# Dilated attention in a decoder layer: 32 tile products replaced by 8 full-array products on block-diagonal weights

## The reference

```python
B, N, D = x.shape                                  # 16, 128, 256
w, r, H, hd = (SEG, DILATION, NUM_HEADS, HEAD_DIM) # 64, 2, 16, 16
nseg = Np // w                                     # 2 segments
s = w // r                                         # 32 tokens of a head in a segment
xs = x.reshape(B, nseg, w, H, hd).transpose(0, 1, 3, 2, 4)
offsets = jnp.arange(H) % r                        # even heads see even tokens, odd heads odd ones
idx = offsets[:, None] + jnp.arange(s)[None, :] * r
g = jnp.take_along_axis(xs, idx[None, None, :, :, None], axis=3)
scores = jnp.einsum('bnhqd,bnhkd->bnhqk', g, g) * scale
attn = jax.nn.softmax(scores, axis=-1)
out = jnp.einsum('bnhqk,bnhkd->bnhqd', attn, g)
```

## Time and profile before

| | |
|---|---|
| Median of three executions | 625.38 us |
| Profiled execution: span from its first to its last instruction | 719.4 us |
| Profiled execution: its own time outside that span | not given by the page |
| PE busy in the span | 563.9 us (78%) |
| DVE, ACT, POOL busy | 368.4, 330.1, 390.5 us |
| PE busy from 120 to 180 us (three steps) | 49.2 of 60 us |
| Mean granted clock of TensorE over the span | 0.915 of 2.4 GHz |

### The profile page before, as it was taken

One profiled execution on the slowest core, in us unless ns is written; L12 is line 12 of the kernel. 1 busy time (PEld: TensorE's weight loads), 2 busy tenths in 40 slices (PEclk: granted clock), 3 DMA queues, 4 the chain that ended last, 5 costly groups with the idle time before them and its releaser, 6 DMA issues.

```text
span 719.4 us, 17476 instructions
## 1 busy us (share of the span) xinstructions
PE 563.9 (78%) x5097; PEld 414.4 (58%) x5098; DVE 368.4 (51%) x1527; ACT 330.1 (46%) x1204; POOL 390.5 (54%) x599
## 2 busy tenths in 40 slices
PE   3768787888878888888306889988998888985995
PEld 2445454544555554444105777777777776774884
DVE  1537566666677566666402444444444444443453
ACT  2445555455455455456003555555555554553012
POOL 5443445545544455545551666766666666665432
PEclk9789999999999899999556999999999999998899
DMA  9999996111111111112285554555555454554994
GB/s 206 277 275 365 342 339 231 69 59 73 68 50 64 55 73 73 65 66 74 99 308 182 155 165 150 160 156 167 152 164 159 143 157 142 164 160 148 425 418 145
DMA packets 83069, 121.31 MB, mean 169 GB/s; under 512 B 13779, under 2 KB 72669, under 8 KB 80992
## 3 DMA queue, kind: packets, MB, share of 16 engines
q1 hardware_dynamic: 64128, 78.46, 36.3%
q0 software_dynamic: 14016, 38.44, 14.7%
q10 hardware_dynamic: 4896, 4.03, 1.7%
HBM read 56.07 MB, written 69.01 MB: 174 GB/s over the span
## 4 chain that ended last, share of the span: by engine, by line
PE 54%; issue 12%; ACT 12%; DVE 9%; DMA 6%; ACTq 3%; POOL 2%; SPq 1%; another core or an unknown queue 0%; DVEq 0%; POOLq 0%
PE bank L793 14%; PE bank L809 9%; ACT pr L870 7%; PE bank L611 5%; PE bank L785 5%; PE bank L601 4%; PE bank L803 3%; PE bank L661 3%; DMA out<-fin 3%; PE bank L744 2%; DMA wall<-results 2%; DVE nmax L1024 2%; PE bank L619 2%; ACTq L296 1%; DVE tg L1218 1%
## 5 line engine op out<-in xcount | busy, mean ns | idle before, releaser
L556 POOL DMA_INDIRECT results<-ys,wcol x152 | 150.1, 988 | 25.8 <-POOL pscrap L545 22.0
L530 POOL DMA_INDIRECT queues<-x,xidx x128 | 129.1, 1009 | 36.9 <-issue 36.5
L793 PE MATMUL bank<-wall,xtT 128*128 x616 | 127.1, 330 | 0.7 <-issue 0.7
L870 ACT ACTIVATE pr<-bank,nmax 128x128 f32<-128x128 f32 x256 | 90.9, 370 | 29.1 <-DVE nmax L1024 29.1
L1218 DVE SCALAR_TENSOR_TENSOR tg<-th,bank 128x96 f32<-128x96 f32 x154 | 39.1, 254 | 125.3 <-ACT th L957 96.9
L793 PEld LDWEIGHTS bank<-wall,xtT 128*128 128x128 f32 x616 | 98.4, 194 | 1.4 <-issue 1.3
L963 ACT ACTIVATE ys<-bank,wcol 128x256 f32<-128x256 f32 x152 | 71.9, 473 | 54.6 <-PE bank L809 36.6
L809 PE MATMUL bank<-wall,hT 96*128 x304 | 94.5, 392 | 0.0
L785 PE MATMUL bank<-ident,xt 128*128 128x128 f32 x310 | 63.3, 286 | 35.4 <-DMA xt<-queues 24.1
L785 PEld LDWEIGHTS bank<-ident,xt 128*128 128x128 f32 x310 | 59.0, 197 | 49.9 <-DMA xt<-queues 25.1
L876 ACT COPY prT<-bank 128x512 f32<-128x512 f32 x64 | 38.5, 601 | 88.9 <-PE bank L611 86.2
(11 more groups left out here) (178 smaller groups left out, 947.2 us busy)
## 6 DMA issues: line engine op xcount, KB each, us to landing
xt<-queues SPq DMA_DIRECT2D x162, 160.0 KB
results<-zeros SPq DMA_DIRECT2D x16, 1024.0 KB
wall<-results SPq DMA_DIRECT2D x16, 1024.0 KB, 12.7
queues<-zeros SPq DMA_DIRECT2D x32, 160.0 KB, 4.9
wall<-in_L_ffn_w_gate SPq DMA_DIRECT2D x4, 768.0 KB
wall<-in_L_ffn_w_up SPq DMA_DIRECT2D x4, 768.0 KB
wall<-in_L_ffn_w_down SPq DMA_DIRECT2D x4, 768.0 KB
results<-ys,wcol POOLq DMA_INDIRECT x152
```

The costliest lines, as they stand in the source:

```text
L530: pool.indirect_dma_start(xg, bass.IndirectOffsetOnAxis(ap=xidx[:, par, k:k + 1], axis=0), x2[:, par, :], None, bounds_check=last_row, oob ...
L556: pool.indirect_dma_start(yr, bass.IndirectOffsetOnAxis(ap=wcol[:, u, 1:2], axis=0), ys[:, u, :], None, bounds_check=last_y, oob_is_err=Fa ...
L793: ins = pe.matmul(bank[2 + u % 2][:, 0:2 * INTER].rearrange("p (g i) -> p g i", g=2), xtT[:, u % 2, kk, :], wall[:, bass.ds(e, GU)].rearrange(
L870: ins = act.activation(pr[:, g % 2, q, :], pS[g % 2][:, q * P:(q + 1) * P], ACT.Exp, bias=nmax[:, 4 * g + q:4 * g + q + 1], accum_out=den[ ...
```

## The change

`eAT` becomes 128 partitions x 8 pairs x 128 columns and is set to zero once, on POOL, among the constants (one more constant, so `B_CONST` goes from 27 to 28). DVE transposes with four instructions, one for each partition group, each writing its 32x32 blocks to the columns of its own group, so that `eAT[:, j, :]` is block-diagonal. In step 0 DVE waits for `B_CONST` first. PE then forms the sums of a pair for all four groups with one product over the full array: stationary `eAT[:, j, :]` (128x128), moving the 32 columns of `gm`. The other places of the 128x128 operand are zero. The scores (L640) stay as they are.

```diff
-B_CONST = FIRST_CONST + 23
-N_CONST = 49
+B_CONST = FIRST_CONST + 24
+N_CONST = 50
...
-        eAT = sb("eAT", [P, PAIRS, GR])
+        eAT = sb("eAT", [P, PAIRS, P])
...
+            put(pool.memset, eAT[:, :, :].rearrange("p j k -> p (j k)"), 0.0)
             put(pool.memset, kP[:, :, :, :, :].rearrange("p a m q k -> p (a m q k)"), 0.0)
...
                     for j in range(PAIRS):
-                        for g in range(NG):
-                            ins = pe.matmul(pA[GR * g:GR * (g + 1), j * 32:(j + 1) * 32],
-                                            eAT[GR * g:GR * (g + 1), j, :],
-                                            gm[GR * g:GR * (g + 1), par, j * 32:(j + 1) * 32],
-                                            start=True, stop=True, tile_position=(GR * g, GR * g))
+                        ins = pe.matmul(pA[:, j * 32:(j + 1) * 32], eAT[:, j, :], gm[:, par, j * 32:(j + 1) * 32],
+                                        start=True, stop=True)
                     ins.then_inc(peA.sem, 1)
...
                     dve.reciprocal(rA[:, :], dA[:, :]).then_inc(s, 1)
-                    dve.transpose(flat2(eAT), flat2(eA)).then_inc(s, 1)
+                    if isinstance(a, int) and a == 0:
+                        dve.wait_ge(consts, B_CONST)
+                    for g in range(NG):
+                        rows = slice(GR * g, GR * (g + 1))
+                        ins = dve.transpose(eAT[rows, :, GR * g:GR * (g + 1)], eA[rows, :, :])
+                    ins.then_inc(s, 1)
```

## The result

The kernel with the change takes 661.16 us (median of four executions, 660.92 to 661.41), the kernel before beside it on the same chip 625.78 us (624.9 to 626.59). The ratio is 1.0572, with a 95% interval from 1.0556 to 1.0587: 35.4 us slower. The forecast was 648.5 us, within 630 to 660. The direction is right, the size is not, and 661.16 lies outside the range.

The account below looks back on a forecast made before the run. The chain V0, L661, T1, ACT's copy, exponentials, T2 and next scores was taken to set each step. 15 steps x 1.2 us (1.08 + 0.15, rounded) = 18.0, plus step 0's 5.1: 625.4 + 23.1 = 648.5 us, range 630 to 660.

Parts of the forecast that it names:

- The drip: L661's passes in small bursts with 0.45 us issue gaps, steps 3 to 15; taken as recording's price, absent from timed runs.
- The rival beside which the Trainium skill's: L661's slow bursts are the kernel's own, perhaps instruction fetches, and 96 fewer instructions end them: 600 us, chance 0.14.
- The span of 697 us: Forecast length of the changed kernel's profiled execution, shorter than the 719 us before, though the timed kernel takes longer.
- PE's products: In L661, 16 passes at 0.11 us, 1.76 us, replace 0.68, so T1 comes 1.08 us later each step.
- DVE's transposes: Three more ahead of yB at 0.32 us each: yB 0.96 to 1.31 us later, 0.96 taken; V0 0.15 later.
- the slack of V0: About a microsecond between yB and V0's start, used up by the transposes; V0 then 0 to 0.4 us later.
- The half clock: PE's stretch at clock 0.50 following L661, seen in the first profile; forecast to be gone after the change.
- half clock in all steps: Rival: L661's products run at half clock in every step, 3.55 us, 2.9 later instead of 1.1; 675 us, chance 0.04.
- Step 0: First step: zeroing 0.95 us, transposes 1.35, passes at half clock 2.8 more; sum 5.1 us.
- POOL's path: POOL's root of r and indirect DMAs, moved by the transposes' 0.96; bounds the step's cost from below, 0.96 to 1.5 us.
- the shift is hidden: Rival: POOL's indirect DMAs set the pace and PE's 1.1 us lies beside them; no change, chance 0.04.

Follow-up runs that it names:

- The repeat: The kernel before, profiled once more without an edit; 624.90 us, ratio 0.9994, span 622.9 us.
- experiment 10: The kernel before, unchanged, profiled once more; 624.90 us, ratio 0.9994, span 622.9 us.
- experiment 1: Kernel before with four 32-partition transposes in place of one, the 32 tile products kept; 644.13 us, ratio 1.0312.
- experiment 9: Kernel before with its one 128-partition transposition issued four times, three into tiles that nothing reads; 637.89 us, ratio 1.0187.
- Experiment 11: Changed kernel with three bf16 products of 512 columns on PE ahead of its wait for the transposes; 657.21 us, ratio 1.0505.
- experiment 6: Changed kernel, eAT zeroed on DVE, yB ahead of the four transposes, PE's wait for them moved behind V0; 648.04 us, ratio 1.0346.
- experiment 8: Kernel before with yB ahead of the one transposition on DVE, PE untouched; 627.27 us, ratio 1.0024.
- the two parts: Four transposes alone on the kernel before, 644.13 us; full-array products alone (changed kernel, one transposition, eAT zeroed on DVE), 641.94 us.
- experiment 3: Changed kernel with eAT zeroed by DVE at the start instead of by POOL among the constants; 659.69 us, ratio 1.0547.
- experiment 12: Kernel before with POOL's second root taken after five of a step's eight indirect DMAs, not six; 626.79 us, ratio 1.0004.

## Why the prediction was right about the direction and wrong about the size

**The drip is not the kernel's** (right, but for a reason that failed). It was left out of the sum as a price of recording. The repeat has none with recording on, and its span is the timed one. So it belonged to that one execution, and not to recording as such; what stretched it stays open. That the conclusion held all the same was in part luck, and the direction of the forecast hung on it. The rival beside which the Trainium skill's "Runtime: NRT & Kernel Launch", section "Instruction fetch mechanics", was named falls with it: the loop's branches are in experiment 10 too, and L661 has no such gaps there. The span of 697 us forecast for the profile after rested on the drip and is void.

**PE's products** (right). Forecast 16 x 0.11 = 1.76 us, measured 1.81, with no gaps of issue. Against 0.68 this was to be 1.08 a step; the clean trace has 0.92 for the 64 passes, so it is 0.89. The forecast was too high here by 0.19 x 15 = 2.9 us, which hides a part of what it had too low elsewhere. Forecast 2.9 to 3.0 us from V0 to the copy of T1, measured 2.84, and 3.03 one step earlier. The drain that the Trainium skill's "TensorEngine Tiling (Array Packing)", section "Key Properties", names was left out of the sum, and it has no row of its own here. From V0's start to L661's it is 0.36 us before and after, but V0 stands on tiles of 128x32, so the mode changes behind it in both kernels; the switch that fell away, from L661 to T1, lies inside the 0.92, and no run prices it.

**DVE's transposes** (wrong, and this is the step that failed). The prediction had both spacings, 0.32 from the 128-partition transposition and 0.44 from copies on 32 partitions, and took 0.32 as "the operation's own". The new instructions have the 0.44. `yB` is late by 1.44 us instead of 0.96, and since the slack of V0 was used up by then, all that is more goes to V0: 0.74 instead of the 0.15 taken from a range that ended at 0.4. That is 0.59 x 15 = 9 us, the largest part of the miss. The upper end of the range missed as well: 1.31 is three pieces at 0.44, but it is four at 0.44 less one at 0.32, and the 0.15 us from `yB`'s end (127.84) to V0's start (127.99) was not counted. Experiments 1 and 9 show the same split by themselves, 1.44 against 0.97.

**The half clock** (wrong). I said that the stretch of half clock after L661 would go, because PE gets busier. It went with the drip, and the change brings its own, 3.4 us in about every second step (row 107.70:111.10 and the one behind it). Experiment 11 prices it at 4 us. The rival "half clock in all steps" meant the passes themselves; from step 2 on they run at full clock and what follows is slow (the S3 products, L602, take 1.91 us at 112.28 and 1.02 at 126.01 in the same trace). I had it at 4 in 100.

**Step 0** (right in the sum, its parts off in opposite ways). Forecast 5.1 us: 0.95 for the zeroing, 1.35 for the transposes, 2.8 for the slow passes. Measured 5.45 at `oA`: PE starts L661 at 18.31 instead of 15.36, 2.95 later and not 2.3, since the four transposes take 1.78 us, and 2.5 more pass from there to `oA`, not 2.8.

**POOL's path** (right that it carries the transposes, not that this is all). It was named as a bound of 0.96 to 1.5 from below. Experiments 1 and 6, where PE's path has room, have a period of 1.42 and 1.43 more. In the change PE's path is longer. The rival "the shift is hidden" fell: the median rose by 35.4 us.

The sum by the measured terms: 15 x (0.74 + 0.89) = 24.5, step 0 5.4, half clock 4, together 34 of the 35.4 us. The 1.5 us left may lie behind the steps: from the last indirect DMA of the first phase to the first expert block it is 24.39 us after the change (342.31 to 366.70) and 22.81 in the repeat of before (307.62 to 330.43), where a long stretch at half clock lasts 47.8 and 44.3 us. But experiments 8 and 9, without the change, have 24.28 and 24.36 with 47.8, so it need not be the change's. Singly the two parts cost 19.2 and 17.0 us, 2.2 of the latter in step 0, and together 34.7 (experiment 3, beside them). This looks additive but isn't a step's reading: the 1.42 of the first is POOL's path, the 0.82 of the second PE's, and the 2.14 of both is PE's path again, with 0.74 of the transposes and the half clock in it.

## What to carry to other kernels

Profile the unchanged kernel again when its span stands far above the timed runs, before pricing anything by it. Where an instruction is split by partitions, price the pieces by a row with as few partitions, not by the same operation on all 128. Where two paths end together, a change costs the longer of what it adds to each (here PE's 0.74 + 0.89 = 1.63 us a step against POOL's 1.44), and not the sum; ask of a new wait on PE also what it does to the clock of the work behind it.

## What the runs showed of the hardware

- A DVE transposition in 32x32 blocks of 32 partitions x 256 fp32 stands 0.44 us from the next one, that of 128 partitions x 256 0.32 us. Whether the destination is strided makes no difference (0.39 and 0.39 us). Why the smaller one takes longer was not tried.
- From the first of L661's 64 passes of 32x32 to T1 it took 0.68 to 0.69 us in experiments 1 and 9 and 0.85 to 1.16 in experiments 8, 10 and 12 from step 3 on, V0 ahead of them in both cases. PE had waited ahead of V0 in the first two, but by 0.17 us only in some steps, and step 6 of experiment 10 has 0.93 behind a wait of 0.21. What decides it is left open.
- A wait of 0.7 to 0.9 us, then V0 and the 16 passes of 32 columns, was followed by 3.4 us at 1.2 GHz in about every second step; three products of 512 columns in that wait kept the clock at 2.4 GHz.
- One profiled execution took 96.5 us more than another of the same kernel.
- In the first 28 us the granted clock can read 1.00 while the passes run at half pace: two S2 products took 1.91 us at 24.26 in experiment 10 and 1.02 us later in the same trace.
